# Attention scores of two graphs in opposite halves of the matmul array, with the PSUM banks dealt out anew

## The chip, the cores and the metric

The kernel runs on one core of a Trainium2 chip. The metric is the time of one execution on the device in microseconds (us). The core's engines are called PE (TensorE, matrix multiplications; its weight loads are shown apart as PEld), DVE (VectorE), ACT (ScalarE), POOL (GpSimd) and SP (SyncE, which issues most transfers). Each engine works through its own list of instructions in order and waits on semaphores that other engines raise. PE's results go to PSUM, here eight banks of 512 float32 values on each of 128 partitions; DVE and ACT read it, POOL does not in this kernel.

## What is computed

Two layers of graph attention with 12 heads over 128 graphs of 64 nodes and 384 features, each followed by a residual and a layer norm. Cut to what matters here:

```python
# layer 0 (and layer 1 with other weights, bias = adj, and an output product Wo, bo)
q, k, v = x @ Wq + bq, x @ Wk + bk, x @ Wv + bv          # split into 12 heads of 32
scores = q @ k.T / sqrt(32) + beta * adj                  # per graph and head: 64 x 64
scores = where(adj > 0, scores, -9e15)
probs = softmax(scores, axis=-1)
out = probs @ v                                           # heads, 64 x 32 each
x = layernorm(x + out)
```

All of it is float32 or split float32: a product of activations and weights is made as three products of a high part and a low part (`split_product`).

## The kernel before

The rows are cut into 16 chunks of 512 rows, a chunk into four tiles of 128 rows, which is two graphs. `ORDER` is the list of 32 phases: a phase attends one chunk in one layer, and after the first three the layers take turns, layer 1 of chunk c and then layer 0 of chunk c+3. A phase has four steps, one for each tile (`STEPS`), so there are 128 tiles, numbered 0 to 127 in the text. Every engine runs the same list of steps, software-pipelined: in a step `cur` is the tile whose scores are made, `prev` (one earlier) has its probabilities transposed and multiplied by v, `last` (two earlier) gets its result and residual, `done` (three earlier) is normalised. `units` are products of nine matmuls that make q, k or v of the next phase, two or three in a step, and `turned` is the tile two phases ahead whose activations are made ready as a high and a low part. Layer 0 reads these from memory (`xt_in`); layer 1 turns the normalised output of layer 0 on PE.

On PE a step is: scores(cur), turned activations (layer 1 only), first unit, result(last), transposes of prev's probabilities, other units, heads(prev). DVE: bias add and row maxima of cur (with a second maximum in layer 1), normalise(done), low part of the turned tile, residual of last, v units, row sums of cur, low part of the heads (layer 1). In the last step of a layer-0 phase DVE also prepares the next chunk's bias (`make_bias0`). POOL subtracts the row maximum (`shift`) and multiplies by the reciprocal sum (`scale`), two large operations a tile. ACT makes the high parts, the exponentials, and copies out of PSUM.

The scores of a tile are 24 matmuls of 32 rows by 64 columns, the heads 24 of 64 rows by 32 columns; as float32, each is two weight loads and two multiplications in the profile, hence x48. Their place in the array follows from their operands: the rows from the partitions of the inputs, the columns from the partitions of the output. In the scores, head `hh` of a group of four uses rows 32·hh and column half `hh % 2`, for both graphs alike:

```python
half_of, par = hh // 2, hh % 2
ps_s[par * NODES:(par + 1) * NODES, half_of, at_key:at_key + NODES]
```

PSUM is dealt out as two banks for scores (`ps_s`), two for the units (`ps_u`), two shared by the transposed probabilities and the heads (`ps_p`), one for the turned activations (`ps_x`) and one for the results (`ps_o`).

## Time and profile before

| | us |
|---|---|
| median of 3 runs | 1102.79 (1102.42 to 1103.21) |
| the profiled execution | 1102.04 |
| its span, first to last instruction | 1100.2 |
| PE busy | 1061.6 (96%) |
| PE weight loads busy | 916.5 (83%) |
| DVE busy | 936.5 (85%) |
| POOL busy | 529.2 (48%) |
| ACT busy | 445.3 (40%) |

Matmuls overlap each other and their recorded ends are modelled, so a busy PE is not PE at its peak; starts tell more than durations. The granted TensorE clock was 0.992 of full speed over the span. A row of the timeline gives a start in us from the span's start, a length, the engine, the line of the kernel, the operation, output and inputs, their shapes, and a count where neighbours are merged; in brackets stands the idle time ahead of it and what ended it. A row of waits names who waited for whom, the sum in us, how often, and the longest. A row of the chain gives a start, the length that the chain spent there, and what it was.

### The profile page before, as it was taken

What the parts mean: (1) busy time and instruction counts of PE and PEld (TensorE: products, weight loads), DVE (VectorE), ACT (ScalarE), POOL (GpSimd) and SP (SyncE); (2) the same over time, 40 slices, a digit from 0 to 9 for tenths busy, and PEclk for the clock granted to TensorE, in tenths of its full rate; (3) what the DMA queues carried; (4) which work ended last, traced back from release to release, by engine and by line L of the source; (5) the groups of instructions that cost most, each with busy time, mean ns of one, the idle gap of its engine ahead of it and who ended that gap; (6) DMA issues with size and microseconds to landing.
All of it is one profiled execution on the core that took longest, in us unless ns stands there. A gap on an engine that the chain in (4) does not pass through costs nothing.

```text
span 1100.2 us, 38267 instructions
## 1 busy us (share of the span) xinstructions
PE 1061.6 (96%) x16896; PEld 916.5 (83%) x16896; DVE 936.5 (85%) x1642; ACT 445.3 (40%) x713; POOL 529.2 (48%) x454
## 2 busy tenths in 40 slices
PE   6789999999999999999999999999999999999975
PEld 5678888888888888888888888888888888888864
DVE  4468998989989898898989989898998989878786
ACT  4334434433444344444434344343343434444321
POOL 0235554554545445364554645455364544655443
PEclk9899999999999999999999999999999999999998
DMA  8211211202111111211201111111211210010101
GB/s 271 64 40 36 74 31 49 60 20 61 38 43 59 43 38 46 65 38 43 59 30 51 46 40 56 42 42 42 65 38 43 59 41 11 17 36 2 36 29 37
DMA packets 61749, 53.32 MB, mean 48 GB/s; under 512 B 35984, under 2 KB 55440, under 8 KB 61584
## 3 DMA queue, kind: packets, MB, share of 16 engines
q1 hardware_dynamic: 60752, 49.69, 15.3%
q8 instruction: 134, 2.20, 0.8%
q10 hardware_dynamic: 832, 1.18, 0.3%
q14 instruction: 31, 0.25, 0.1%
HBM read 38.28 MB, written 12.58 MB: 46 GB/s over the span
## 4 chain that ended last, share of the span: by engine, by line
PE 90%; DVE 4%; issue 2%; ACT 1%; DMA 1%; POOL 1%; ACTq 0%; POOLq 0%; DVEq 0%
PE ps_u L346 53%; PE ps_s L363 9%; PE ps_o L346 8%; PE ps_p L431 7%; PE ps_p L446 7%; PE ps_x L376 3%; PE ps_o L460 2%; DVE probs L628 1%; POOL probs L766 1%; DMA k_sb<-in_wk 1%; DVE row_sum L678 1%; DVE xt_lo L656 1%; ACT probs L553 0%; DMA xt_in<-in_x_t 0%; DVE row_max L638 0%
## 5 line engine op out<-in xcount | busy, mean ns | idle before, releaser
L766 POOL TENSOR_TENSOR probs<-probs,row_max 128x768 f32<-128x768 f32 x128 | 209.8, 1639 | 314.9 <-DVE row_max L638 314.9
L772 POOL TENSOR_TENSOR probs<-probs,row_inv 128x768 f32<-128x768 f32 x128 | 188.9, 1475 | 127.1 <-DVE row_inv L686 69.2
L522 ACT COPY probs_t<-ps_p 128x768 f32<-128x768 f32 x128 | 102.7, 802 | 201.9 <-PE ps_p L431 201.8
L346 PE MATMUL ps_u<-w_hi_v,xt_lo 128*128 128x384 f32 x384 | 137.9, 359 | 5.0 <-DVE v_sb L671 5.0
L553 ACT ACTIVATE probs<-probs 128x768 f32<-128x768 f32 x128 | 108.3, 846 | 83.5 <-POOL probs L766 83.4
L678 DVE TENSOR_REDUCE row_sum<-probs 128x12 f32<-128x768 f32 x128 | 121.5, 949 | 23.9 <-ACT probs L553 23.1
L787 POOL TENSOR_TENSOR rstd<-var_eps,minus_half 128x1 f32<-128x1 f32 x128 | 70.3, 549 | 125.5 <-DVE var_eps L719 125.5
L346 PE MATMUL ps_u<-w_hi_v,xt_hi 128*128 128x384 f32 x384 | 129.7, 338 | 0.0
L346 PE MATMUL ps_u<-w_lo_v,xt_hi 128*128 128x384 f32 x384 | 129.3, 337 | 0.0
L346 PE MATMUL ps_u<-xt_hi,w_lo_k 128*128 128x512 f32 x288 | 119.1, 414 | 4.9 <-DVE v_sb L671 4.9
L346 PE MATMUL ps_u<-xt_hi,w_lo_q 128*128 128x512 f32 x285 | 121.7, 427 | 1.7 <-ACT q_sb L541 0.9
L638 DVE TENSOR_REDUCE row_max<-probs 128x12 f32<-128x768 f32 x128 | 121.3, 948 | 2.2
L363 PE MATMUL ps_s<-k_sb,q_sb 32*64 32x64 f32 x6144 | 118.7, 221 | 0.8 <-ACT k_sb L543 0.8
L346 PE MATMUL ps_u<-xt_hi,w_hi_k 128*128 128x512 f32 x288 | 113.9, 395 | 0.0
L346 PE MATMUL ps_u<-xt_lo,w_hi_k 128*128 128x512 f32 x288 | 113.1, 393 | 0.0
L346 PE MATMUL ps_u<-xt_hi,w_hi_q 128*128 128x512 f32 x285 | 112.1, 393 | 0.0
L363 PEld LDWEIGHTS ps_s<-k_sb,q_sb 32*64 32x64 f32 x6144 | 101.0, 132 | 13.1 <-ACT k_sb L543 1.2
L656 DVE TENSOR_TENSOR xt_lo<-xt_in,xt_hi 128x384 fp32r<-128x384 f32 x60 | 101.8, 1697 | 11.7 <-ACT xt_hi L516 11.7
L346 PE MATMUL ps_u<-xt_lo,w_hi_q 128*128 128x512 f32 x285 | 111.4, 391 | 0.0
L446 PEld LDWEIGHTS ps_p<-probs_t,v_sb 64*32 64x32 f32 x6144 | 72.2, 106 | 44.8 <-issue 36.9
L431 PE MATMUL ps_p<-ident,probs 128*128 128x128 f32 x768 | 105.9, 274 | 0.4 <-POOL probs L772 0.4
L446 PE MATMUL ps_p<-probs_t,v_sb 64*32 64x64 f32 x6144 | 92.9, 224 | 6.2 <-ACT probs_t L522 6.2
(78 smaller groups left out, 2031.3 us busy)
## 6 DMA issues: line engine op xcount, KB each, us to landing
x_in<-in_x SPq DMA_DIRECT2D x16, 768.0 KB, 4.6
out<-z SPq DMA_DIRECT2D x64, 192.0 KB, 1.9
xt_in<-in_x_t SPq DMA_DIRECT2D x15, 768.0 KB, 4.6
adj<-in_adj SPq DMA_DIRECT2D x64, 128.0 KB, 2.9
xt_in<-in_x_t SPq DMA_DIRECT2D x3, 256.0 KB, 4.7
q_sb<-in_wq ACTq DMA_DIRECT2D x3, 192.0 KB, 4.9
k_sb<-in_wk ACTq DMA_DIRECT2D x1, 576.0 KB, 7.9
v_sb<-in_wv SPq DMA_DIRECT2D x1, 576.0 KB, 7.7
```

Source lines behind the costliest of these rows:

```text
L346: last = nc.tensor.matmul(dst, a(g), b(g), start=(g == 0 and n == 0), stop=(g == KT - 1 and n == 2))
L363: last = nc.tensor.matmul(ps_s[par * NODES:(par + 1) * NODES, half_of, at_key:at_key + NODES], q_sb[p][rows, g, GT * t + b, :], k_sb[p][ro ...
L431: last = nc.tensor.transpose(ps_p[:, i // KT, (i % KT) * P:(i % KT + 1) * P], probs[t % 2][:, i, :, :], ident[:])
L446: last = nc.tensor.matmul(ps_p[hh * HD:(hh + 1) * HD, b, g * NODES:(g + 1) * NODES], v_sb[p][keys, t, h * HD:(h + 1) * HD], probs_t[keys, ...
L522: nc.scalar.copy(probs_t[:].rearrange("p (a i) n -> p a (i n)", a=2), ps_p[:, :, 0:KT * P]).then_inc(probs_t_ready, 1)
L553: nc.scalar.activation(e, e, ACT.Exp).then_inc(exp_ready, 1)
L638: nc.vector.tensor_reduce(row_max[t % 2][:], rows, AX_X, ALU.max).then_inc(max_ready, 1)
L656: nc.vector.tensor_tensor(xt_lo[p][:, :, t * P:(t + 1) * P], src, xt_hi[p][:, :, t * P:(t + 1) * P].bitcast(F32), ALU.subtract).then_inc(x ...
L678: nc.vector.reduce_sum(row_sum[p][:], probs[p][:].rearrange("p i b k -> p (i b) k"), AX_X)\
L766: nc.gpsimd.tensor_tensor(s, s, over_keys(row_max[p]), ALU.subtract).then_inc(shifted, 1)
L772: nc.gpsimd.tensor_tensor(s, s, over_keys(row_inv[p]), ALU.mult).then_inc(probs_ready, 1)
L787: nc.gpsimd.tensor_tensor(rstd[p][:], var_eps[p][:], minus_half[:], ALU.pow).then_inc(rstd_ready, 1)
```

## The change

The scores of the two graphs of a tile (`b`) go to opposite column halves: `side = (hh % 2) ^ b`. So the 24 matmuls use all eight 32x64 tiles of the array in turn, where they used four. `ps_s` grows to four banks, bank `half_of * GT + b`, and the transposed probabilities of the tile before go into its first two; the heads, the results and the turned activations share two banks, `ps_h`. The waits follow: scores wait for ACT's copy of the transposed probabilities of two tiles earlier, the transposes wait for DVE's bias add of the current tile, the heads for the residual's read of the result and for the low part of the turned tile. The turned activations move behind the result on PE; ACT and DVE take the first unit, and DVE the residual, ahead of the turned tile. DVE adds the bias in two instructions, one for each graph.

```diff
-        ps_s = ps("ps_s", [P, 2, 512])
+        ps_s = ps("ps_s", [P, 4, 512])
         ps_u = ps("ps_u", [P, 2, 512])
-        ps_p = ps("ps_p", [P, GT, 512])
-        ps_x = ps("ps_x", [P, 512])
-        ps_o = ps("ps_o", [P, 512])
+        ps_h = ps("ps_h", [P, GT, 512])
...
                 if at(tile) > 0:
                     pe.wait_ge(biased, at(tile))
+                if at(tile) > 1:
+                    pe.wait_ge(probs_t_ready, at(tile) - 1)
...
-                            half_of, par = hh // 2, hh % 2
-                            at_key = (g * GT + b) * NODES
+                            half_of, side = hh // 2, (hh % 2) ^ b
                             last = nc.tensor.matmul(
-                                ps_s[par * NODES:(par + 1) * NODES, half_of, at_key:at_key + NODES],
+                                ps_s[side * NODES:(side + 1) * NODES, half_of * GT + b, g * NODES:(g + 1) * NODES],
...
-            def turn_activations(tile):
+            def heads_read(tile):
+                pe.wait_ge(o_t_ready, at(tile) + 1)
+                if tile[0] == 1:
+                    pe.wait_ge(o_lo_ready, second_no(tile))
+
+            def turn_activations(tile, last_heads):
...
-                pe.wait_ge(xt_lo_ready, TURN_NO[tile] - 1)
+                heads_read(last_heads)
...
-            def turn_probs(tile):
+            def turn_probs(tile, scored):
                 pe.wait_ge(probs_ready, at(tile) + 1)
-                if at(tile) > 0:
-                    pe.wait_ge(o_t_ready, at(tile))
-                earlier = tile_before(tile, 1)
-                if earlier and earlier[0] == 1:
-                    pe.wait_ge(o_lo_ready, second_no(earlier))
+                if scored:
+                    pe.wait_ge(biased, at(scored) + 1)
...
-            def heads(tile):
+            def heads(tile, turned):
...
                 pe.wait_ge(probs_t_ready, at(tile) + 1)
+                if at(tile) > 0:
+                    pe.wait_ge(z_ready, at(tile))
+                if turned and turned[0] == 1:
+                    pe.wait_ge(xt_lo_ready, TURN_NO[turned])
...
-                s = probs[t % 2]
-                keys = GT * NODES
-                nc.vector.tensor_tensor(
...
+                for b in range(GT):
+                    done = nc.vector.tensor_tensor(
+                        s[:, :, b, :].rearrange("p (a g) k -> p a g k", a=2),
+                        ps_s[:, b::GT, 0:KT * NODES].rearrange("p a (g k) -> p a g k", g=KT),
+                        bias[:, GT * t + b, :].unsqueeze(1).unsqueeze(1).to_broadcast([P, 2, KT, NODES]), ALU.add)
+                done.then_inc(biased, 1)
...
+                for unit in s.units[:1]:
+                    unit_out(unit)
+                if s.last:
+                    residual(s.last)
                 if s.turned:
                     activations_lo(s.turned)
-                if s.last:
-                    residual(s.last)
-                for unit in s.units[:1]:
-                    unit_out(unit)
```

On PE, in the step of tile 60 (the first of a layer-1 phase; `o_t` are the last tile's heads, `probs` the probabilities of tile 59), between the first unit and the transposes, before:

```order
L346 MATMUL ps_u<-xt_hi,w_hi_q 128x512
L460 MATMUL ps_o<-ident,o_t 128x128 [waits o_t_ready,z_ready]
L460 MATMUL ps_o<-ident,o_t 128x128 x2
L431 MATMUL ps_p<-ident,probs 128x128 [waits o_t_ready,probs_ready]
L431 MATMUL ps_p<-ident,probs 128x128 x5
```

and changed:

```order
L346 MATMUL ps_u<-xt_hi,w_hi_q 128x512
L465 MATMUL ps_h<-ident,o_t 128x128 [waits o_t_ready]
L465 MATMUL ps_h<-ident,o_t 128x128 x2
L382 MATMUL ps_h<-ident,x_1 128x128 [waits o_t_ready,normed]
L382 MATMUL ps_h<-ident,x_1 128x128 x2
L434 MATMUL ps_s<-ident,probs 128x128 [waits biased,probs_ready]
L434 MATMUL ps_s<-ident,probs 128x128 x5
```

The turned activations (`x_1`) now stand here, and the transposes wait for `biased`, the bias add of tile 60.

On PE, from the heads of tile 58 into the step of tile 60, before:

```order
L446 MATMUL ps_p<-probs_t,v_sb 32x64 [waits v_ready,probs_t_ready]
L446 MATMUL ps_p<-probs_t,v_sb 32x64 x23
L363 MATMUL ps_s<-k_sb,q_sb 64x64 [waits biased,qk_ready]
L363 MATMUL ps_s<-k_sb,q_sb 64x64 x23
L376 MATMUL ps_x<-ident,x_1 128x128 [waits xt_lo_ready,normed]
L376 MATMUL ps_x<-ident,x_1 128x128 x2
L346 MATMUL ps_u<-xt_hi,w_lo_q 128x512 [waits xt_lo_ready,v_ready]
```

and changed:

```order
L453 MATMUL ps_h<-probs_t,v_sb 32x64 [waits v_ready,z_ready,probs_t_ready]
L453 MATMUL ps_h<-probs_t,v_sb 32x64 x23
L364 MATMUL ps_s<-k_sb,q_sb 64x64 [waits probs_t_ready,biased,qk_ready]
L364 MATMUL ps_s<-k_sb,q_sb 64x64 x23
L346 MATMUL ps_u<-xt_hi,w_lo_q 128x512 [waits xt_lo_ready,v_ready]
```

The turned activations have left the place behind the scores, and the heads and the scores have each one more wait.

On DVE, in the step of tile 59 (the last of a layer-0 phase), before:

```order
L628 TENSOR_TENSOR probs<-ps_s,bias 128x768 [waits probs_turned,bias0_ready,scores_made]
L638 TENSOR_REDUCE row_max<-probs 128x12 [waits biased]
L644 TENSOR_SCALAR x_2<-z,mean_var,rstd 128x384 [waits rstd_ready]
L656 TENSOR_TENSOR xt_lo<-xt_in,xt_hi 128x3x128 [waits xt_loaded,xt_hi_ready]
L712 TENSOR_TENSOR z<-ps_o,x_in 128x384 [waits x_loaded0,stored1,o_made]
L714 BN_STATS stats<-z 128x6 [waits z_ready]
L717 BN_AGGR mean_var<-stats 128x2 [waits stats_ready,const_set]
L719 TENSOR_SCALAR var_eps<-mean_var 128x1 [waits mean_ready]
L671 TENSOR_TENSOR v_sb<-ps_u,bv_rows 128x384 [waits unit_made]
L678 TENSOR_REDUCE row_sum<-probs 128x12 [waits exp_ready]
```

and changed:

```order
L632 TENSOR_TENSOR probs<-ps_s,bias 128x6x64 [waits probs_turned,bias0_ready,scores_made]
L632 TENSOR_TENSOR probs<-ps_s,bias 128x6x64
L641 TENSOR_REDUCE row_max<-probs 128x12 [waits biased]
L647 TENSOR_SCALAR x_2<-z,mean_var,rstd 128x384 [waits rstd_ready]
L674 TENSOR_TENSOR v_sb<-ps_u,bv_rows 128x384 [waits unit_made]
L715 TENSOR_TENSOR z<-ps_h,x_in 128x384 [waits x_loaded0,stored1,o_made]
L717 BN_STATS stats<-z 128x6 [waits z_ready]
L720 BN_AGGR mean_var<-stats 128x2 [waits stats_ready,const_set]
L722 TENSOR_SCALAR var_eps<-mean_var 128x1 [waits mean_ready]
L659 TENSOR_TENSOR xt_lo<-xt_in,xt_hi 128x3x128 [waits xt_loaded,xt_hi_ready]
L681 TENSOR_REDUCE row_sum<-probs 128x12 [waits exp_ready]
```

The bias add is in two, the v unit and the residual stand ahead of `xt_lo`, the low part of the turned tile.

## Rows read from the trace of the kernel before

**Rows 1.** The page: busy time by engine; the chain's shares by line.

```profile
PE 1061.6 (96%) x16896; PEld 916.5 (83%) x16896; DVE 936.5 (85%) x1642; ACT 445.3 (40%) x713; POOL 529.2 (48%) x454
...
PE ps_u L346 53%; PE ps_s L363 9%; PE ps_o L346 8%; PE ps_p L431 7%; PE ps_p L446 7%; PE ps_x L376 3%; PE ps_o L460 2%; DVE probs L628 1%; POOL probs L766 1%; DMA k_sb<-in_wk 1%; DVE row_sum L678 1%; DVE xt_lo L656 1%; ACT probs L553 0%; DMA xt_in<-in_x_t 0%; DVE row_max L638 0%
```

**Rows 2.** The waits, whole span, PE and its weight loads.

```profile
PE ps_u L346 <- DVE v_sb L671: 10.7, 5, 4.3
...
PEld ps_p L431 <- POOL probs L772: 3.9, 15, 0.6
PEld ps_u L346 <- ACT k_sb L543: 2.9, 13, 0.2
```

**Rows 3.** The chain of work that ended last, 520 to 540 us.

```profile
521.19 0.65 PE ps_p L446 x45
521.85 0.86 PE ps_s L363 x48
...
524.81 0.66 PE ps_p L431 x6
...
529.05 2.21 PE ps_u L346 x9
531.26 0.33 PE ps_o L460 x3
```

**Rows 4.** Stretches, line L446 (heads) alone: stretch, length, PE and PEld busy (records).

```profile
505.10:505.15 0.05, 0.02 (x4) 0.03 (x4) 1.00 0.00 0
...
505.10:505.30 0.20, 0.17 (x22) 0.17 (x30) 1.00 0.00 0
505.10:505.40 0.30, 0.27 (x33) 0.28 (x34) 1.00 0.00 0
...
505.10:505.66 0.56, 0.53 (x48) 0.54 (x48) 1.00 0.00 0
```

**Rows 5.** Stretches, line L363 (scores) alone, the same columns.

```profile
505.75:506.05 0.30, 0.27 (x16) 0.27 (x20) 1.00 0.00 0
...
505.75:506.50 0.75, 0.72 (x48) 0.72 (x48) 1.00 0.00 0
```

**Rows 6.** Lines L363 and L446: records, ns at least, in the median and at most.

```profile
L363 PEld LDWEIGHTS ps_s<-k_sb,q_sb x6144: 127/133/133, 22.9 to 1075.3; 32*64 32x64 f32 x199
...
L446 PEld LDWEIGHTS ps_p<-probs_t,v_sb x6144: 102/106/169, 47.3 to 1090.5; 64*32 64x32 f32 x199
L446 PE MATMUL ps_p<-probs_t,v_sb x6144: 212/216/309, 47.3 to 1090.6; 64*32 64x64 f32 x199
```

**Rows 7.** Timeline of tiles 59 and 60: PE's scores, DVE and POOL.

```profile
521.78 0.93 PE L363 MATMUL ps_s<-k_sb,q_sb 32*64 32x64 f32 x48
...
522.77 0.96 DVE L628 TENSOR_TENSOR probs<-ps_s,bias 128x768 f32<-128x768 f32 x1 [0.29 <-PE ps_s L363]
...
524.80 1.64 POOL L766 TENSOR_TENSOR probs<-probs,row_max 128x768 f32<-128x768 f32 x1 [1.63 <-DVE row_max L638]
...
525.02 1.83 DVE L656 TENSOR_TENSOR xt_lo<-xt_in,xt_hi 128x384 fp32r<-128x384 f32 x1
526.77 0.55 DVE L712 TENSOR_TENSOR z<-ps_o,x_in 128x384 f32<-128x384 f32 x1
...
527.64 0.93 PE L363 MATMUL ps_s<-k_sb,q_sb 32*64 32x64 f32 x48
...
530.05 1.48 POOL L772 TENSOR_TENSOR probs<-probs,row_inv 128x768 f32<-128x768 f32 x1 [1.04 <-DVE row_inv L682]
530.31 1.50 DVE L596 TENSOR_SCALAR bias<-adj 128x512 f32<-128x512 f32 x1
...
532.52 0.95 DVE L628 TENSOR_TENSOR probs<-ps_s,adj 128x768 f32<-128x768 f32 x1
```

**Rows 8.** Line L656, layer 0's form: ns at least, in the median and at most.

```profile
L656 DVE TENSOR_TENSOR xt_lo<-xt_in,xt_hi x60: 549/1829/1832, 16.0 to 919.1; 128x384 fp32r<-128x384 f32 x60
```

**Rows 9.** Groups by line: the bias add (busy us, mean ns of one).

```profile
L628 DVE TENSOR_TENSOR probs<-ps_s,bias 128x768 f32<-128x768 f32 x64 | 60.8, 951 | 16.1 <-PE ps_s L363 15.9
```

More of the change, by code:

```diff
@@ L373, in turn_activations @@
                 pe.wait_ge(normed, at((0, c, t)) + 1)
-                pe.wait_ge(xt_lo_ready, TURN_NO[tile] - 1)
+                heads_read(last_heads)
                 for g in range(KT):
-                    last = nc.tensor.transpose(ps_x[:, g * P:(g + 1) * P], x1[c % 3][:, t, g * P:(g + 1) * P],
+                    last = nc.tensor.transpose(ps_h[:, 1, g * P:(g + 1) * P], x1[c % 3][:, t, g * P:(g + 1) * P],
                                                ident[:])
@@ L420, in make_unit @@
                 last.then_inc(unit_made, 1)
[L422 removed]
+            def turn_probs(tile, scored):
                 pe.wait_ge(probs_ready, at(tile) + 1)
[L424 to L428 removed]
+                if scored:
+                    pe.wait_ge(biased, at(scored) + 1)
                 t = tile[2]
                 for i in range(PAIRS):
[L431 removed]
+                    last = nc.tensor.transpose(ps_s[:, i // KT, (i % KT) * P:(i % KT + 1) * P],
                                                probs[t % 2][:, i, :, :], ident[:])
                 last.then_inc(probs_turned, 1)
[L435 removed]
+            def heads(tile, turned):
                 layer, c, t = tile
@@ L444, in heads @@
                             h = g * HG + hh
-                            half_of, par = hh // 2, hh % 2
+                            half_of, side = hh // 2, (hh % 2) ^ b
                             last = nc.tensor.matmul(
-                                ps_p[hh * HD:(hh + 1) * HD, b, g * NODES:(g + 1) * NODES],
+                                ps_h[hh * HD:(hh + 1) * HD, b, g * NODES:(g + 1) * NODES],
                                 v_sb[p][keys, t, h * HD:(h + 1) * HD],
-                                probs_t[keys, half_of * KT + g, par * NODES:(par + 1) * NODES],
+                                probs_t[keys, half_of * KT + g, side * NODES:(side + 1) * NODES],
                                 start=True, stop=True)
@@ L454, in result @@
                 layer = tile[0]
-                if at(tile) > 0:
-                    pe.wait_ge(z_ready, at(tile))
-                pe.wait_ge(o_t_ready, at(tile) + 1)
+                heads_read(tile)
                 if layer == 0:
                     for g in range(KT):
-                        last = nc.tensor.transpose(ps_o[:, g * P:(g + 1) * P], o_t[:, g, :], ident[:])
+                        last = nc.tensor.transpose(ps_h[:, 0, g * P:(g + 1) * P], o_t[:, g, :], ident[:])
                 else:
@@ L463, in result @@
                         pe.wait_ge(w_lo_ready, w_count["o1"])
-                    pe.wait_ge(o_lo_ready, second_no(tile))
                     last = split_product(
-                        ps_o[:, 0:D], lambda g: o_hi[:, g, :], lambda g: o_lo[:, g, :],
+                        ps_h[:, 0, 0:D], lambda g: o_hi[:, g, :], lambda g: o_lo[:, g, :],
                         lambda g: w_hi["o1"][:, g, :], lambda g: w_lo["o1"][:, g, :])
@@ L473, in _ @@
                     scores(s.cur)
-                if s.turned:
-                    turn_activations(s.turned)
                 for unit in s.units[:1]:
@@ L479, in _ @@
                     result(s.last)
+                if s.turned:
+                    turn_activations(s.turned, s.last)
                 if s.prev:
-                    turn_probs(s.prev)
+                    turn_probs(s.prev, s.cur)
                 for unit in s.units[1:]:
@@ L484, in _ @@
                 if s.prev:
-                    heads(s.prev)
+                    heads(s.prev, s.turned)
         @block.scalar
@@ L626, in bias_and_max @@
                 s = probs[t % 2]
-                keys = GT * NODES
-                nc.vector.tensor_tensor(
-                    s[:].rearrange("p (a g) b k -> p a g (b k)", a=2),
-                    ps_s[:, :, 0:KT * keys].rearrange("p a (g n) -> p a g n", g=KT),
-                    bias[:, GT * t:GT * t + GT, :].rearrange("p b k -> p (b k)").unsqueeze(1).unsqueeze(1)
-                    .to_broadcast([P, 2, KT, keys]),
-                    ALU.add).then_inc(biased, 1)
+                for b in range(GT):
[4 more added lines that the diff above has]
+                done.then_inc(biased, 1)
                 dve.wait_ge(biased, at(tile) + 1)
@@ L654, in activations_lo @@
                 else:
[L655 removed]
+                    src = ps_h[:, 1, 0:D].rearrange("p (g n) -> p g n", g=KT)
                 nc.vector.tensor_tensor(
@@ L711, in residual @@
                     old = x1[c % 3][:, t, :]
-                nc.vector.tensor_tensor(z[p][:], ps_o[:, 0:D], old, ALU.add).then_inc(z_ready, 1)
+                nc.vector.tensor_tensor(z[p][:], ps_h[:, 0, 0:D], old, ALU.add).then_inc(z_ready, 1)
                 dve.wait_ge(z_ready, at(tile) + 1)
@@ L732, in _ @@
                     normalise(s.done)
+                for unit in s.units[:1]:
+                    unit_out(unit)
+                if s.last:
+                    residual(s.last)
                 if s.turned:
                     activations_lo(s.turned)
-                if s.last:
-                    residual(s.last)
-                for unit in s.units[:1]:
-                    unit_out(unit)
                 if s.cur:
```

10 lines of the change are left out of this document (4 added, 6 removed).

## The prediction

> **What bounds the kernel now.** I read the page's shares and its chain of work first: TensorE (PE) is busy 96%, and by line the scores hold 9% of the chain that ends last, the heads 7% [rows 1]. Next the list of waits: PE's largest, 10.7 us for VectorE's (DVE's) `v_sb`, is five waits in the first phases; in the steady part its weight loads lose 2.9 us to ScalarE's copy of `k` and 3.9 us to GpSimd's probabilities, 13 and 15 times [rows 2]. So a microsecond saved on PE is a microsecond, until another engine is late; DVE, busy 85%, is the candidate. I therefore follow the place where DVE is latest: the last tile of a layer-0 phase, here tile 59 by its number, and tile 60, the first of the layer-1 phase behind it [rows 3, 7]. The reader is to see there that DVE starts tile 60's bias add 4.9 us after its scores began (532.52 against 527.64) and PE does not care, since nothing on PE needs that add within the step.
>
> **The scores.** A tile's scores take 0.86 us of the chain, its heads 0.65 [rows 3], both 48 weight loads and 48 multiplications. The scores run at one pace: 16 multiplications begun by 506.05, all 48 by 506.50 [rows 5]: 0.058 us for a round of four, one for each of the four array tiles in turn. The heads have eight array tiles and two paces: 30 loads by 505.30, only 34 by 505.40, the last 14 until 505.6 [rows 4]. I read this as a limit on work in flight: 32 pairs are ready at the start, the next enter only as the first multiplications end (0.22 to 0.24 us after they start, [rows 6]), and then some 17 ns apart for two pairs. The change gives the scores eight array tiles too: four row groups by two column halves, each (bank, half) written by one row group. By the heads' pattern the scores' 48 would begin within 0.51 us; their load is 27 ns longer (133 against 106, [rows 6]) and stands twice in that path: 0.565 us, where 0.71 is spent now. That is 0.145 us a tile, 128 times: **-18.6 us**. Bounds: 0 if the second four do not run beside the first; 0.21 if they get as quick as the heads; 0.33 if no limit in flight exists (six rounds of 0.058 fewer, less the longer start). I take 0.145, since the heads are the nearest row: same count, eight tiles, same element type.
>
> **DVE's side.** The bias add becomes two of 384 elements a partition. One of 768 takes 0.95 us [rows 9]; one of 384 from PSUM 0.55, and it begins 0.08 before the end of an independent neighbour (526.77 against 525.02 + 1.83, [rows 7]). The pair costs 0.55 - 0.08 + 0.55 = 1.02, +0.07 us a tile. Against that `activations_lo` moves behind `residual`. Its layer-0 form, with two inputs from SBUF, takes 0.55 us at best, 1.83 in the median [rows 8]: at 525.02 it starts inside GpSimd's subtraction (524.80 to 526.44) and ends 0.4 us after it [rows 7]. Behind `residual` it begins about 5.1 us after the scores, and that subtraction ends about 4.6 after them. I take 0.55, so -1.28 us of DVE a tile in layer-0 phases. None of this is on PE's path by itself.
>
> **The new waits.** The transposes now go into the scores' banks, so PE's transposes of tile k-1 wait until DVE has read tile k's scores. At tile 59 that is hidden: the read ends 0.85 + 1.02 = 1.9 us after the scores begin, the transposes come 2.8 after (524.81 less 521.85, less 0.145, [rows 3]). At tile 60 it is not. Now: bias add 59 starts 0.99 us after scores 59, bias add 60 another 9.75 later, DVE working without a pause between [rows 7]. Changed: 0.85, then 9.75 - 1.28 + 0.07 = 8.54, then 1.02 for the halves: 10.41 us after scores 59 begin. Scores 60 follow scores 59 by 5.86 - 0.145 = 5.72, so the read ends 4.69 after scores 60 begin; an end on another engine has reached PE 0.05 later elsewhere in the trace. PE is there after 0.715 (scores), 2.21 (unit), 0.33 (result, [rows 3]) and 0.33 (turned activations, now here, like the result three transposes) = 3.58. It waits **1.16 us**. Queued behind that wait on PE are the transposes, two units and the heads, and ScalarE's copies and GpSimd's next tile wait for those. There are 13 layer-1 phases behind a layer-0 phase that prepares the next bias (1.50 us at 530.31, inside GpSimd's multiplication from 530.05, which stays): **+15.1 us**. Bounds of the wait: 0.1 if that preparation escapes the collision, 2.4 if `xt_lo` does not escape its own.
> The heads wait for `z` and for the turned tile's low part. Both follow the result by DVE's residual chain, and the heads follow it by the transposes and at least one unit. Only in the last step of a layer-1 phase, whose units are the short `v` ones and whose DVE work holds both maxima, do I put the low part late, by 0.28 us, 14 times: **+3.9 us**, an estimate with bounds 0 and 7.
> What vanishes: the waits of PE's loads for `k` and for the probabilities [rows 2], both at tile 60 and the one behind it, where DVE is then 1.2 us earlier: **-6.8 us** (bound: half of it). The turned activations cost 0.30 us behind the scores and 0.33 like any three transposes, 64 times: **+1.5 us**. Their wait for ScalarE's copy of the last heads is one that the result has just made, and the scores' wait for the copy of the turned probabilities one that the heads ahead of them made: nothing. ScalarE's changed order follows PE's, and it is idle more than half the time. SP's load of the next `xt_in` waits for the last `xt_lo`, 0.6 us later than now, a phase ahead of its use.
> Start and end: the `v_sb` waits of the first phases shrink, since `v_sb` goes ahead of the residual and `xt_lo`, while the new waits appear there too, as DVE is late; in the last tiles, which have no units, `z` takes the place of the copy of the probabilities as the heads' last wait. Together I put them at **+1.5 us**, bounds -8 and +6.
>
> **The sum**: -18.6 + 15.1 + 3.9 - 6.8 + 1.5 + 1.5 = -3.4 us on the profiled execution's 1102.0, so 1098.6. The median of the runs lies 0.75 above that execution; that and the half microsecond by which such sums are uncertain make **1100 us**, 0.25% below before. One late read per pair of phases eats nearly all that PE gains.
>
> **Rivals.** *Tiles without a limit*: the scores save 0.33, not 0.145. Tiles where PE waits for DVE anyway gain nothing, so some 92 of 128 gain 0.185 more, -17 us: **1083 us**. For it speaks the scores' own round of 0.058, against it the heads' slow second pace.
> *The scores do not get shorter* (slower): calls five to eight use the row groups of the first four, with the other columns. If a load cannot run beside a multiplication of its own row group, the rounds stay as they are and the waits remain: +18.6, less some 5.6 at the tiles that wait for DVE anyway (26 in the steady part, 0.145 each, and a dozen in the first phases): **1113 us**. Against it: four loads and four multiplications of the heads have begun within 0.03 us [rows 4], and those four calls share one row group of 64 rows. The Trainium skill, TensorE: Matmul & The Clock Gate, Part 3, under The mechanism, states just that rule: a load overlaps running multiplications only where the row group differs. The trace of before speaks against it for the heads; by the rule the time would be this rival's.
> *`xt_lo` stays slow* (slower): if in the last tile of a layer-0 phase it still starts within a long GpSimd operation, the 1.28 us return to the chain ahead of tile 60, whose wait becomes 2.4 us: 13 x 1.28 = +16.6, **1117 us**. It decides at 0.5 us: by so much GpSimd's subtraction would have to end later, or the residual be done earlier.
>
> **How the numbers follow.** Chances: forecast 0.50 (its own range 1095 to 1106), no limit 0.18, scores unchanged 0.16, slow `xt_lo` 0.16. About 0.2% (2.2 us) can be told from no change: below 1100.6 or above 1105.0. The forecast's half splits into 0.27 below, 0.18 within and 0.05 above; the first rival is faster, the other two are slower but for 0.02 within: 0.45, 0.20, 0.35. The range 1084 to 1115 leaves out half of the first rival and half of the last.
>
> **What would show it.** In the profile after: the scores' piece of the chain at 0.71 instead of 0.86 (0.53 or 0.86 by the rivals); among PE's waits a new line, the transposes for DVE's bias add, of some 15 us with longest waits near 1.2 in the steady part, and one of the heads for `xt_lo`; the layer-0 `xt_lo` at a median of 0.55; the transposes' waits for GpSimd gone. The prediction is wrong if the scores measure outside 0.65 to 0.78, or if the transposes wait in other steps than the first of a layer-1 phase.

## The result

The changed kernel takes 1105.22 us (median of 20 runs, 1101.38 to 1110.94), the kernel before, run beside it, 1102.03 (20 runs, 1100.47 to 1103.42). The ratio is 1.0035, with an interval of 1.002 to 1.005: a little slower, where I had forecast a little faster (1100.0). The time lies in the stated range; the sign is wrong. The profiled execution took 1105.29, its span is 1103.5.

What stands out beside the medians is the spread: the runs of the kernel before lie within 3 us, those of the changed one within 10.

### The profile page after: what moved, and what is told of

Read it like the earlier page. It is cut to its first block, busy times and chain, and to the rows that moved or that the text cites. A ratio compares the mean times of both kernels' runs of the same rounds, so it can differ in the third digit from the quotient of the medians.

```text
span 1103.5 us, 38490 instructions
## 1 busy us (share of the span) xinstructions
PE 1041.7 (94%) x16896; PEld 900.3 (82%) x16896; DVE 887.6 (80%) x1770; ACT 448.2 (41%) x713; POOL 543.3 (49%) x454
## 4 chain that ended last, share of the span: by engine, by line
PE 69%; DVE 21%; issue 6%; ACT 2%; DMA 1%; POOL 1%; ACTq 0%; DVEq 0%; POOLq 0%
PE ps_u L346 42%; PE ps_h L346 7%; PE ps_h L453 6%; PE ps_s L364 6%; PE ps_s L434 6%; DVE probs L632 5%; DVE row_max L641 3%; DVE bias L600 2%; DVE v_sb L674 2%; DVE row_sum L681 2%; DVE stats L717 2%; DVE xt_lo L659 2%; DVE z L715 1%; PE ps_h L382 1%; PE ps_h L465 1%
## 5 line engine op out<-in xcount | busy, mean ns | idle before, releaser
L526 ACT COPY probs_t<-ps_s 128x768 f32<-128x768 f32 x128 | 102.6, 802 | 131.2 <-PE ps_s L434 131.2
L346 PE MATMUL ps_u<-w_hi_v,xt_lo 128*128 128x384 f32 x384 | 137.9, 359 | 0.0
L346 PE MATMUL ps_u<-w_hi_v,xt_hi 128*128 128x384 f32 x384 | 129.6, 338 | 0.0
L346 PE MATMUL ps_u<-w_lo_v,xt_hi 128*128 128x384 f32 x384 | 129.3, 337 | 0.0
L346 PE MATMUL ps_u<-xt_hi,w_lo_q 128*128 128x512 f32 x285 | 122.3, 429 | 2.5 <-issue 2.1
L434 PE MATMUL ps_s<-ident,probs 128*128 128x128 f32 x768 | 105.9, 274 | 19.7 <-DVE probs L632 19.7
L346 PE MATMUL ps_u<-xt_hi,w_lo_k 128*128 128x512 f32 x288 | 118.2, 411 | 3.4 <-ACT q_sb L545 3.4
L790 POOL TENSOR_TENSOR rstd<-var_eps,minus_half 128x1 f32<-128x1 f32 x128 | 84.3, 659 | 72.0 <-DVE var_eps L722 72.0
L453 PEld LDWEIGHTS ps_h<-probs_t,v_sb 64*32 64x32 f32 x6144 | 72.6, 106 | 56.3 <-issue 45.4
L346 PE MATMUL ps_u<-xt_hi,w_hi_k 128*128 128x512 f32 x288 | 112.9, 392 | 0.0
L346 PE MATMUL ps_u<-xt_lo,w_hi_q 128*128 128x512 f32 x285 | 112.2, 394 | 0.6 <-issue 0.6
L346 PE MATMUL ps_u<-xt_lo,w_hi_k 128*128 128x512 f32 x288 | 112.3, 390 | 0.0
L346 PE MATMUL ps_u<-xt_hi,w_hi_q 128*128 128x512 f32 x285 | 112.2, 394 | 0.0
L453 PE MATMUL ps_h<-probs_t,v_sb 64*32 64x64 f32 x6144 | 92.8, 224 | 17.1 <-ACT probs_t L526 9.2
L434 PEld LDWEIGHTS ps_s<-ident,probs 128*128 128x128 f32 x768 | 88.5, 141 | 24.9 <-issue 23.8
L364 PE MATMUL ps_s<-k_sb,q_sb 32*64 32x64 f32 x6144 | 99.8, 232 | 0.8 <-ACT k_sb L547 0.8
L364 PEld LDWEIGHTS ps_s<-k_sb,q_sb 32*64 32x64 f32 x6144 | 82.2, 131 | 13.1 <-ACT k_sb L547 1.2
```

The source lines that it names most:

```text
L346: last = nc.tensor.matmul(dst, a(g), b(g), start=(g == 0 and n == 0), stop=(g == KT - 1 and n == 2))
L364: last = nc.tensor.matmul(ps_s[side * NODES:(side + 1) * NODES, half_of * GT + b, g * NODES:(g + 1) * NODES], q_sb[p][rows, g, GT * t + b, :],
L434: last = nc.tensor.transpose(ps_s[:, i // KT, (i % KT) * P:(i % KT + 1) * P], probs[t % 2][:, i, :, :], ident[:])
L453: last = nc.tensor.matmul(ps_h[hh * HD:(hh + 1) * HD, b, g * NODES:(g + 1) * NODES], v_sb[p][keys, t, h * HD:(h + 1) * HD], probs_t[keys, ...
L526: nc.scalar.copy(probs_t[:].rearrange("p (a i) n -> p a (i n)", a=2), ps_s[:, 0:2, 0:KT * P]).then_inc(probs_t_ready, 1)
L790: nc.gpsimd.tensor_tensor(rstd[p][:], var_eps[p][:], minus_half[:], ALU.pow).then_inc(rstd_ready, 1)
```

## The profile after

The page's busy times first, then four of PE's waits (sum in us, times, longest), against [rows 1, 2].

```profile
PE 1041.7 (94%) x16896; PEld 900.3 (82%) x16896; DVE 887.6 (80%) x1770; ACT 448.2 (41%) x713; POOL 543.3 (49%) x454
```

```profile
PE ps_s L434 <- DVE probs L632: 19.7, 19, 1.7
...
PE ps_h L453 <- DVE xt_lo L659: 7.8, 17, 1.5
...
PE ps_u L346 <- issue: 2.7, 3, 1.6
...
PEld ps_u L346 <- DVE v_sb L674: 0.4, 1, 0.4
```

PE is busy 20 us less and DVE 49 us less, and the kernel is no faster. The two waits that the prediction named are there, the transposes (L434) for the bias add (L632) and the heads (L453) for the low part (L659). The loads' waits for `k` and for the probabilities [rows 2] no longer appear, and that for `v_sb` has shrunk to one of 0.4 us. A third line was in no part of my sum: 2.7 us in which PE's units (L346) waited for nothing that the profile shows ("issue").

**The scores** are what the prediction said. The chain of the changed kernel around tile 59 and 60, and the stretches of tile 59's scores alone (line L364; stretch, length, PE and PEld busy with their counts), which answer to [rows 3, 5]:

```profile
517.42 0.66 PE ps_h L453 x45
518.08 0.72 PE ps_s L364 x45
...
527.37 1.02 DVE probs L632 x2
528.39 0.14 issue
528.53 0.85 PE ps_s L434 x6
```

```profile
518.00:518.05 0.05, 0.04 (x6) 0.04 (x7) 1.00 0.00 0
...
518.00:518.30 0.30, 0.29 (x32) 0.29 (x33) 1.00 0.00 0
518.00:518.40 0.40, 0.39 (x36) 0.39 (x37) 1.00 0.00 0
```

0.72 us on the chain where 0.71 was forecast. The scores now have the heads' two paces: 32 multiplications and 33 loads by 518.30, only four more in the next 0.10 us. In the first 0.05 us seven loads and six multiplications have begun. In the kernel before it is four of each, one for each of its four array tiles, and the fifth load begins 0.055 us after the first (the two passes of a call don't stand side by side; the first four multiplications last 265 ns each there, here the first eight, those behind them 217):

```profile
521.75:521.80 0.05, 0.02 (x4) 0.02 (x4) 1.00 0.00 0
```

So calls five and six run beside the first four although they share their row groups, in other columns, and by 0.30 us 32 multiplications have begun instead of 16 [rows 5]. The Trainium skill (TensorE: Matmul & The Clock Gate, Part 3, The mechanism) says that a load overlaps running multiplications only where the row group differs; here the trace differs from it, and the measurement decides: another column half is enough.

**The wait at tile 60** is also what the prediction worked out. The timeline of DVE and PE there (columns as in [rows 7]):

```profile
523.15 0.56 DVE L659 TENSOR_TENSOR xt_lo<-xt_in,xt_hi 128x384 fp32r<-128x384 f32 x1
...
523.74 0.78 PE L364 MATMUL ps_s<-k_sb,q_sb 32*64 32x64 f32 x48
...
525.16 1.51 DVE L600 TENSOR_SCALAR bias<-adj 128x512 f32<-128x512 f32 x1
...
528.53 0.85 PE L434 MATMUL ps_s<-ident,probs 128*128 128x128 f32 x6 [1.08 <-DVE probs L632]
```

The bias add ends 4.65 us after tile 60's scores began (528.39 against 523.74; forecast 4.69) and PE waits 1.08 us (forecast 1.16). `xt_lo` behind the residual takes 0.56 us instead of 1.83 [rows 8], and the preparation of the bias still collides with GpSimd and takes 1.5.

**Step by step.** The length of each step of the steady part, from the start of one tile's scores to the next in the traces, is the best table for the whole study. Tiles 56 to 59 are a layer-0 phase, 60 to 63 the layer-1 phase behind it; the columns on the right are experiments below.

| step of tile | before | after | E1 four tiles | E2 bias later | E4 both edits | E7 before, new order | E9 low part first |
|---|---|---|---|---|---|---|---|
| 56 | 10.16 | 10.00 | 10.13 | 9.98 | 10.02 | 10.16 | 9.99 |
| 57 | 8.10 | 7.95 | 8.11 | 7.95 | 7.95 | 8.10 | 7.95 |
| 58 | 7.90 | 7.74 | 7.89 | 7.74 | 7.74 | 7.90 | 7.74 |
| 59 | 5.87 | 5.73 | 5.83 | 5.71 | 5.71 | 5.87 | 6.69 |
| 60 | 9.50 | 10.34 | 10.42 | 9.06 | 9.06 | 9.15 | 10.66 |
| 61 | 7.39 | 7.01 | 7.19 | 7.62 | 7.03 | 7.13 | 7.01 |
| 62 | 9.45 | 9.35 | 9.50 | 9.36 | 9.35 | 9.45 | 9.35 |
| 63 | 7.34 | 7.71 | 7.71 | 7.70 | 7.28 | 7.34 | 7.70 |
| pair of phases | 65.71 | 65.83 | 66.78 | 65.13 | 64.14 | 65.10 | 67.09 |

Every layer-0 step is 0.14 to 0.16 shorter, tile 60 is 0.84 longer, 61 is 0.38 shorter (its old waits are gone), 63 is 0.37 longer: gain and loss in a pair cancel.

**The stops.** Three steps of the profiled execution are longer than their like: tile 29 (7.84), 69 (7.89) and 70 (12.68), where their like take 7.03, 7.03 and 9.35. That is 0.8 + 0.9 + 3.3 = 5.0 us. The chain there, and stretches of all engines around the third stop (the column behind POOL is the granted clock; then DMA share and GB/s):

```profile
600.69 1.13 PE ps_u L346 x4
601.82 0.59 issue
602.41 1.42 PE ps_u L346 x5
...
608.58 0.89 PE ps_u L346 x3
609.47 1.61 issue
611.08 2.38 PE ps_u L346 x6
```

```profile
607.50:609.40 1.90, 1.90 (x82) 1.52 (x67) 1.60 (x6) 0.89 (x2) 1.14 (x1) 1.00 0.74 274
609.40:611.00 1.60, 0.07 (x1) 0.00 (x0) 1.57 (x4) 0.00 (x0) 0.34 (x1) 1.00 0.00 0
611.00:614.80 3.80, 3.72 (x11) 3.24 (x11) 1.14 (x2) 0.69 (x1) 1.64 (x1) 0.57 0.02 4
```

In the third stop PE halts in the middle of a unit whose operands it has been using for a microsecond, stays idle 1.6 us, and then has a granted clock of 0.57 in the mean until 614.8, most of that stretch at the lower of the two levels (1.2 of 2.4 GHz). This stop itself is half of its price; behind the two short ones the clock stays at 1.00. No engine releases PE there, so I looked at its own stream of instructions. Those arrive over a queue of their own, here in the page's list of queues (packets, MB, share), then the list of all queues for 590.1 to 600.0 us and for 593.9 to 600.0 alone:

```profile
q8 instruction: 134, 2.20, 0.8%
```

```profile
DMA packets 400, 0.79 MB, mean 79 GB/s; under 512 B 16, under 2 KB 16, under 8 KB 400
```

```profile
DMA packets 0, 0.00 MB, mean 0 GB/s; under 512 B 0, under 2 KB 0, under 8 KB 0
```

134 blocks in the span are one per 8.2 us, and 257 of PE's 34,405 instructions each (33,792 loads and multiplications, 613 that mostly wait). Counted in the trace's order, PE has begun 7,873, 18,625 and 18,881 instructions when it stops, each time 193 more than a multiple of 256, and the next one begins 1.3 to 1.5 us after a block has landed (at 270.6, 600.9 and 609.8). All idle times of PE of 0.3 us and more without a releaser in the experiments' traces stand at this place of the count too, but for E9's 13 at the heads. In the kernel before a block lands at least 3.8 us before PE reaches that place. So PE stops because it has run out of instructions. Ahead of the second stop the queues carry data until 593.9, then nothing at all for six microseconds, and only then the block: no other transfer held it up. The Trainium skill (Runtime: NRT & Kernel Launch, Terms) says that an engine's instruction memory is refilled in 16 KiB blocks; the trace agrees (each of the 134 packets has 16,384 bytes).

## The experiments

**E1, four array tiles in the changed kernel.** Scores and heads use the old column half:

```diff
-                            half_of, side = hh // 2, (hh % 2) ^ b
+                            half_of, side = hh // 2, hh % 2
```

> The changed kernel with the two graphs of a tile in the same column half again, so the scores use four array tiles as before; banks, waits and orders stay those of the change. My theory: the scores go back from 0.72 to 0.86 us a tile, 0.14 us at each of the some 95 tiles where PE does not wait for VectorE anyway (not the first and last of a layer-1 phase): +13 to +15 us on the changed kernel's 1105, so about 1119. Rival, the eight tiles in use at once are what stops PE's stream of instructions now and then (0.6 to 4 us a time, the spread of the changed kernel's runs): then the stops go with them, the runs lie within 3 us of each other, and the median is near 1114.

Measured: 1119.45 us (1115.09 to 1121.12), ratio to the kernel before, run beside it as in all that follow, 1.0145 (1.0122 to 1.0169). The scores' piece of the chain:

```profile
518.25 0.86 PE ps_s L364 x48
```

The gain of the eight tiles is real and has the forecast size: 0.10 to 0.18 us in six of eight steps (the first four, 61 and 62), less or nothing where PE waits for DVE. The runs spread over 6 us and one stop of 1.8 us is in its trace, so the stops don't come from the eight tiles.

**E2, the bias prepared later.**

```diff
-                if s.t == 3 and s.cur and s.cur[0] == 0 and s.cur[1] < CHUNKS - 1:
+                if s.t == 3 and s.cur and s.cur[0] == 0 and s.phase < 2:
                     make_bias0(s.cur[1] + 1)
+                if s.t == 0 and s.cur and s.cur[0] == 1 and s.phase > 2:
+                    before = ORDER[s.phase - 1]
+                    if before[0] == 0 and before[1] < CHUNKS - 1:
+                        make_bias0(before[1] + 1)
```

> The changed kernel with the preparation of the next layer-0 bias moved from the end of a layer-0 phase to the end of the first step of the layer-1 phase behind it (the first two phases keep their place). My theory: the first step of a layer-1 phase falls from 10.35 us to about 9.2 since the transposes no longer wait for the bias add, 13 times: -15 us, about 1090; the other steps stay. Rival, VectorE's 1.5 us come back one step later, as a wait of PE there: within 4 us of the changed kernel's 1105.

Measured: 1094.38 us (1092.29 to 1095.27), ratio 0.9921 (0.9905 to 0.9938). Two of its waits on PE:

```profile
PE ps_h L453 <- DVE xt_lo L659: 14.6, 30, 1.5
...
PE ps_s L434 <- DVE probs L632: 4.9, 5, 1.6
```

The step of tile 60 fell by 1.28 us (1.15 expected), and the transposes' wait from 19 times to 5. But the rival had a part: the step of tile 61 grew by 0.61, because the 1.5 us of preparation now stand ahead of that step's `xt_lo`, and the heads wait for it 13 times more. Its trace has a stop of 2.1 us at tile 6.

**E3, the low part earlier.** In layer 1 `xt_lo` stands between the residual's sum and its statistics:

```diff
+                if between and between[0] == 1:
+                    activations_lo(between)
                 dve.wait_ge(z_ready, at(tile) + 1)
```

> The changed kernel with the low part of a layer-1 tile made right behind the residual's sum, ahead of its statistics, so 1 us earlier. My theory: the heads' wait for it in the last step of a layer-1 phase goes, 7.70 to about 7.3 us, 14 times, and some in the first phases: -5 us, about 1100. Rival, the heads are held by the sum itself or by the statistics' consumers: within 2 us of 1105.

Measured: 1100.33 us (1093.44 to 1102.93, 10 runs), ratio 0.9977 (0.9961 to 0.9994). The heads' waits for `xt_lo` fell from 7.8 us, 17 times, to one of 0.4, the last step of a layer-1 phase from 7.71 to 7.28. Its trace has two stops of more than 2 us.

**E4, both edits.**

> Both edits: the bias prepared later and the low part made earlier. My theory: they act on different steps, so the sum, -20 us, about 1085, faster than both kernels. Rival, one takes what the other gives (VectorE is late in both places for one reason): no better than the first edit alone, 1090.

Measured: 1078.82 us (1075.23 to 1087.30), ratio 0.9794 (0.975 to 0.9838): more than the sum, since the wait that E2 created is for the very `xt_lo` that E3 makes early (a pair of phases loses 0.70 us in E2, 0.40 in E3, 1.69 here). The step of tile 61 stays at 7.03. The profiled execution is the slowest of the four, with two stops that make tiles 30 and 70 together 10 us longer. The second of them on the chain, and the stretch behind it (the granted clock stands behind GpSimd's count):

```profile
599.86 0.89 PE ps_u L346 x3
600.75 2.75 issue
603.49 2.72 PE ps_u L346 x6
```

```profile
603.50:606.00 2.50, 2.50 (x6) 1.94 (x6) 0.52 (x2) 0.00 (x0) 1.64 (x1) 0.50 0.02 7
```

**E5, both edits and `x_in` in pieces; E6, the changed kernel with `x_in` in pieces.** The load of 768 KB, in the third step of a layer-1 phase, becomes four of 192 KB, each a step after the residual that frees its rows:

```diff
-                sp.dma_start(x_in[c % 2][:], rows).then_inc(x_loaded[c % 2], 16)
+                sp.dma_start(x_in[c % 2][:, t, :], x_rows[c * CT + t * P:c * CT + (t + 1) * P, :])\
+                    .then_inc(x_loaded[c % 2], 16)
```

> The kernel with both edits (bias prepared later, low part earlier), and the load of x_in, 768 KB at once in the third step of a layer-1 phase, cut into four of 192 KB, each a step after the residual that frees its rows. PE stood still in the run before in two of the third steps (3.38 us at 273.87, 3.14 at 600.35) without waiting for an engine, while that load ran, and at both places a block of its instructions came late. My theory: the big load holds the block up. Then the stops go: spans near 1075, times near 1077 with all runs within 3 us. Rival, the stops have nothing to do with the load: they stay, and the runs spread over 10 us as before (1075 to 1087).

Measured: 1075.85 us (1075.38 to 1076.54), ratio 0.9768 (0.9753 to 0.9782), the lowest median of the study (E11 below is within their scatter).

> The changed kernel with nothing else than the load of x_in in four pieces. Same theory: the stops at tiles 69 and 70 go, the time is 1100 to 1102 with all runs within 3 us, where the changed kernel's runs lie between 1101 and 1111. Rival: they stay, median near 1105.

Measured: 1102.30 us (1100.33 to 1108.65, 10 runs), ratio 1.0015 (1.0001 to 1.003). PE's stops in the two traces, E5 first:

```profile
PE ps_u L347 <- issue: 1.1, 1, 1.1
```

```profile
PE ps_u L347 <- issue: 1.6, 3, 0.8
```

The big load makes some stops longer, but isn't the origin of all: E6 has the same three as the changed kernel, 1.6 us instead of 2.7 in all, the third 0.8 instead of 1.6, and its step of tile 70 falls from 12.68 to 10.31. Its runs still spread over 8 us. The traces tell two kinds of stops apart. In the third steps of layer-1 phases (tiles 30 and 70) the block begins to move only as the load's last packets do (608.7, with packets of the load until 609; in E4 601.0 and 601.1), and those stops last 1.6 to 3.0 us in the changed kernel, E1, E3 and E4, with the load in pieces 1.1 and 0.8. At tiles 29 and 69 of the changed kernel no transfer runs for some six microseconds ahead of the block. Theory and rival each hold half.

**E7, the kernel before with DVE's new order alone.**

```diff
-                if s.turned:
-                    activations_lo(s.turned)
-                if s.last:
-                    residual(s.last)
                 for unit in s.units[:1]:
                     unit_out(unit)
+                if s.last:
+                    residual(s.last)
+                if s.turned:
+                    activations_lo(s.turned)
```

> The kernel before with VectorE's new order alone: v unit and residual ahead of the low part of the turned tile. Nothing else changes, PE's scores stay at 0.86 us. My theory: the low part takes 0.55 us instead of 1.83 in layer-0 phases, so VectorE is early: the waits of PE for v_sb in the first phases (10.7 us) and for the copies and probabilities at the first tiles of layer-1 phases (6.8) go to a large part, -10 to -14 us, about 1090: this edit alone gains more than the whole change. Rival: PE was not held by VectorE, the waits stay or move to others, within 3 us of 1102.

Measured: 1083.25 us (1081.89 to 1086.54), ratio 0.9839 (0.982 to 0.9858). Its low part (ns at least, in the median, at most) and two waits, against [rows 2, 8]:

```profile
L656 DVE TENSOR_TENSOR xt_lo<-xt_in,xt_hi x60: 553/559/1587, 16.2 to 901.7; 128x384 fp32r<-128x384 f32 x60
...
PEld ps_p L431 <- POOL probs L772: 0.2, 1, 0.2
...
PE ps_u L346 <- DVE v_sb L671: 0.7, 2, 0.6
```

This part of the change alone is worth 18 us, more than the 10 to 14 that I expected: the pair of phases gains 0.60 us, 8 us in all, and the stretch up to tile 12, where DVE is PE's bound, goes from 133.5 to 121.2 us. Of these 12.3 us 4.3 lie in the step of tile 0 (16.08 to 11.76): in the kernel before PE waits 4.3 us there for `v_sb`, and the granted clock is 0.50 from 33 to 36 us; in E7 its longest wait there is 2.2 us and the clock stays at 1.00. No stop is in its trace.

**E8, the kernel before with the bias add in two.**

> The kernel before with the bias add in two instructions of 384 elements instead of one of 768. My theory: VectorE pays 0.07 us a tile more, of which PE feels some at the tiles where it waits: +1 to +3 us, about 1105. Rival: the halves overlap fully or are covered, no change.

Measured: 1106.10 us (1105.75 to 1106.94), ratio 1.0043 (1.0027 to 1.006). The 0.07 us a tile on DVE cost PE 4.7 us; its loads wait 16.7 us for `v_sb`, 19 times, where those of the kernel before wait 12.5 us, five times. It is more than the 1 to 3 us expected.

**E9, the low part ahead of unit and residual again**, in layer 0's form only, in the changed kernel:

```diff
+                if s.turned and s.turned[0] == 0:
+                    activations_lo(s.turned)
                 for unit in s.units[:1]:
                     unit_out(unit)
```

> The changed kernel with the low part of the turned tile, layer 0's form only, ahead of the v unit and the residual again, as it stood before. My theory: it starts inside GpSimd's subtraction again and takes 1.83 us, VectorE is 1.28 us later ahead of the first tile of each layer-1 phase, and the transposes' wait there grows from about 1.1 to 2.4 us, 13 times, with more in the first phases: +16 to +20 us, about 1122. Rival: it is fast wherever it stands, because PE and with it VectorE run in another time grid since the change: within 3 us of 1105.

Measured: 1127.46 us (1124.91 to 1131.25), ratio 1.0238 (1.0211 to 1.0264). The last tile of a layer-0 phase on GpSimd, DVE and PE, and two waits of PE:

```profile
534.28 1.64 POOL L771 TENSOR_TENSOR probs<-probs,row_max 128x768 f32<-128x768 f32 x1 [1.48 <-DVE row_max L641]
...
534.50 1.83 DVE L659 TENSOR_TENSOR xt_lo<-xt_in,xt_hi 128x384 fp32r<-128x384 f32 x1
...
536.72 0.55 DVE L715 TENSOR_TENSOR z<-ps_h,x_in 128x384 f32<-128x384 f32 x1
...
537.37 0.71 PE L453 MATMUL ps_h<-probs_t,v_sb 64*32 64x64 f32 x48 [0.87 <-issue]
```

```profile
PE ps_s L434 <- DVE probs L632: 22.6, 18, 1.8
PE ps_h L453 <- issue: 11.8, 13, 1.1
```

The low part starts 0.22 us into GpSimd's subtraction and ends 0.41 us behind it, as in [rows 7]. The Trainium skill (GPSIMD Engine Reference, Specifications) says that GpSimd and VectorE contend where a VectorE instruction has two inputs from SBUF; the trace agrees, 1.83 us inside against 0.56 outside. The price is the one foreseen, 1.26 us a pair, but three quarters of it came back at another place: in tile 59's step the heads wait for the residual's sum (0.96 us more), the rest at tile 60 (0.32). The profile names no releaser for these 13 waits ("issue"), but the heads begin 0.1 us behind the end of that sum, and these gaps are not at the place in PE's count where its blocks end. The time lies 5 us above the 1122 expected; up to tile 12 its trace loses 6.6 us, and it has four stops (0.4 to 2.3 us).

**E10, the kernel before with DVE's new order and the bias later.**

> The kernel before with VectorE's order of the change and the bias prepared later, and nothing of the banks and the eight array tiles. It says what these are worth beside the same VectorE. My theory: like the order alone (1083), less 1 us at most, so 1082 to 1083; what the eight tiles and their banks add is then the 6 to 7 us down to the 1076 of the best so far. Rival: preparing the bias later gains as much here as in the changed kernel (11 us): 1072, and the eight tiles are worth nothing.

Measured: 1084.94 us (1082.61 to 1086.15), ratio 0.9843 (0.9828 to 0.9858), as E7 within their scatter. So the bias preparation costs only where the transposes wait for the bias add, and with nearly the same DVE order the eight tiles and their banks are worth 7 to 9 us (1075.85 against 1083.25 and 1084.94), not 18.6 (E5 also has layer 1's low part earlier and `x_in` in pieces, which E7 and E10 lack): 0.96 a pair is won (65.10 to 64.14), 12 us in all, and the stretch up to tile 12 gives 4 back (125.4 in E5 against 121.2 in E7).

**E11, 64 empty instructions ahead of PE's first unit, in E4's kernel; E12, the same in the changed kernel.** The 129 waits come out as 64 more instructions of PE in the trace (34,469):

```diff
-            pe.wait_ge(ident_ready, 1)
+            for _ in range(129):
+                pe.wait_ge(ident_ready, 1)
```

> The kernel with both edits and x_in loaded at once, with 64 empty instructions (waits that are already satisfied) ahead of PE's first unit, while it waits for the first load. They shift where PE's instruction blocks of 256 begin against the program by a quarter of a block. My theory: the stops belong to the block boundaries, so they move to other instructions of the program (64 instructions earlier) or meet the load no more: 1075 to 1080 with another pattern of stops. Rival, they belong to a place in the program: they stay in the first unit of tiles 30 and 70.

Measured: 1076.70 us (1074.92 to 1078.56), ratio 0.9771 (0.9754 to 0.9788). No step of its trace has a stop; tiles 30 and 70 take 9.35 us.

> The changed kernel with nothing but the 64 empty instructions ahead of PE's first unit. Taking PE's stops without a waiter (0.7, 0.7 and 3.3 us longer steps at tiles 29, 69 and 70) out of its profiled run leaves a span of some 1098.7, a time of 1100.5. My theory: the stops are what set it behind the kernel before, so it comes to 1100 to 1102, its runs within 4 us. Rival: the empty instructions helped the other kernel by chance, or the waits for VectorE alone explain the time: median near 1105 with runs up to 1111.

Measured: 1112.93 us (1105.48 to 1114.74, 5 runs), ratio 1.0105 (1.0088 to 1.0122): a miss, slower by 8 us than without the empty instructions. The stops at tiles 29, 69 and 70 are gone and another one is at tile 45, in the middle of its scores. The chain, and two stretches (columns as above):

```profile
403.74 0.68 PE ps_s L364 x43
404.41 1.45 issue
405.87 0.33 PE ps_s L364 x3
406.19 3.75 PE ps_u L346 x9
```

```profile
404.40:405.80 1.40, 0.01 (x1) 0.00 (x0) 0.00 (x0) 0.00 (x0) 1.04 (x1) 1.00 0.00 0
405.80:410.00 4.20, 4.13 (x14) 3.14 (x15) 3.23 (x5) 0.02 (x1) 0.82 (x1) 0.59 0.01 4
```

So the stops are not tied to a place in the program: shift the blocks, and they sit elsewhere (this one again 193 above a multiple of 256). But they don't vanish by it. The profiled execution was the quickest of the five; the other four, 7 to 9 us longer, have no trace, so what they lost is not shown.

## Why the prediction was wrong, point by point

The step that failed is the sum's list of what holds PE: it has no term for PE's own stream of instructions, which cost 5.0 us in the profiled execution, and it puts the heads' wait for the low part 2.7 us too low. Together that is more than the gain of 3.4 us that was forecast.

- **The scores** (-18.6): right. 0.72 on the chain for 0.71, 0.14 to 0.16 in the steps that feel it, and E1 takes it away again (14.2 us come back; the second rival, which leaves out the tiles where PE waits for DVE anyway, has 13). The limit on work in flight, read from the heads, holds for the scores in the same numbers (32 pairs, then a slow pace). The rivals on both sides of it, no limit and no gain, are out.
- **The wait at the first tile of a layer-1 phase** (+15.1): right. 1.08 for 1.16, at the place named; the step of tile 60 is 0.84 longer where the terms at this place gave 0.8. E2 takes it away.
- **The low part in layer 0** (0.55 for 1.83): right, and E9 shows the rival at 1127 where I had put it at 1117. Its price of 1.28 was right, the place only partly: I had it all at the transposes of tile 60.
- **The heads' wait for the low part** (+3.9, bounds 0 and 7): mis-sized. At tile 63 PE is held 0.49 us (7.71 less the 7.34 - 0.12 that the other terms leave), not 0.28: 13 times 0.21 up to tile 112 is 2.7 us. The prediction works out no path for this term; in the trace DVE is held there by the end of the heads ahead of it:

```profile
549.85 0.67 PE ps_h L453 x45
...
550.54 0.49 ACT o_hi L565
...
551.52 1.02 DVE probs L632 x2
...
556.77 0.48 DVE xt_lo L659
557.25 0.24 issue
557.50 0.72 PE ps_h L453 x40
```

  From the end of the heads (550.52) over ScalarE's `o_hi`, DVE's `o_lo`, the bias add, both maxima and the whole residual to `xt_lo` and the next heads are 7.0 us, while PE has 6.5 of work. A chain through three engines doesn't show in an estimate of how late DVE is alone.
- **Old waits that vanish** (-6.8): right in place; tile 61 is 0.38 shorter, of which 0.12 is the scores less the turned activations.
- **Start and end** (+1.5, bounds -8 and +6, beside some 4 us of the scores' gain in those tiles): better than forecast. Up to tile 12 the trace gained 5.8 us, from tile 112 on it lost 1.3: -4.5 against -2.0 with the scores and the other terms of those tiles counted in. 3.1 of the 5.8 are the step of tile 0 (16.08 to 13.00), where the clock of the kernel before fell behind the wait for `v_sb` (E7) and that of the changed kernel did not: the prediction counts such waits, but no clock behind them.
- **The stops of PE**: no step of the prediction has them; they were put at nothing without a reason. In the profiled execution they are 5.0 of the 6.7 us between the forecast of that execution (1098.6) and its time (1105.29); the rest is 4.1 more in the steady part (2.7 of it at tile 63, 1.4 in small pieces that I assign to nothing) less 2.5 at the ends. By this count the execution would have taken 1100.3 without them. The kernel before shows none, so no row of its trace gave them a size; a list of what holds PE was not complete without its own instructions. That the stops explain the whole spread of the 20 runs is not shown, only that they sit in the trace of one of them and that the lower clock behind the third doubles its price. Two more things are on record. The four quickest of these runs have a mean granted clock of 0.991 to 0.993, the four slowest 0.987 to 0.988. And the step of tile 0 differs between E4 and E11 (14.81 and 11.69 us), which differ in the empty instructions alone: PE waits 3.6 and 2.1 us there behind a load, and in E4 alone the clock then falls (0.56 from 33 to 36 us, against 1.00). How the spread divides between such places is open.

What stays open is why the blocks come late in the kernels of this change and not in the kernel before or in E7, E8 and E10, where one lands at least 3.6 us before PE needs it. Those four have 34,310 instructions of PE instead of 34,405, so their blocks end at other places of the program; whether they would stop too with their blocks shifted was not tried. The big load holds up the blocks of some stops (E5, E6), the place of the block boundary moves the stops (E11, E12); neither explains those at tiles 29, 69 and 45, ahead of which no transfer runs.

## What to carry to other kernels

A step of a producer that nobody waits for becomes the critical path once its buffer is shared: before sharing PSUM banks, follow the reader that will free them through the latest step of the loop, and move what stands ahead of it (here 1.5 us of preparation that could be done one step later) in the same change. Separate the edits of a change and try each alone: here a reordering that was a by-product is worth 18 us by itself, more than the eight array tiles with their new waits, and both together with two more moves on DVE and a load in pieces 26 (1075.85 against 1101.41 for the kernel before beside it). Where a tightly filled engine shows idle time without a releaser, look at its instruction blocks and the clock behind the stop before explaining the time by waits, and count where in the stream the gaps stand: those on the grid of 256 were stops, E9's others were plain waits.

## What the runs showed of the hardware that I had not expected

- PE can run out of instructions: idle 0.3 to 3.0 us, always at the same place in a grid of 256 instructions, until 1.2 to 1.5 us after a block of 16,384 bytes has landed. A long time between two blocks alone does not make a stop: in E11 14 us pass between 515.3 and 529.4, and PE goes on. Behind a stop of 1.6 us the granted clock was 0.57 in the mean of 3.8 us, behind one of 1.45 us 0.59 in the mean of 4.2; behind one of 0.59 us it stayed at 1.00.
- The scores' and heads' loads overlap multiplications in the same row group if their columns differ (seven loads of the scores in 0.05 us over four row groups, where one column half has four).
- With 32 pairs of load and multiplication on the way PE all but stands, as I read it until the first come out: 32 multiplications of a tile's scores begin in the first 0.30 us, four in the next 0.10.
